# Norms of q and k from the products of W and T in place of two Gram diagonals, with ScalarE's passes in a new order

## The chip, the cores and the metric

One core of one Trainium2 chip runs the kernel. The metric is device time in microseconds, the median of several runs; the kernel before has a median of 374.44 us (three runs, 373.13 to 374.47).

## What is computed

The input x is 16 images of 192 channels and 48 x 48 pixels (N = 2304 tokens). Each image is group-normalised, goes through channel attention (8 heads of 24 channels) and is added to x:

```
qkv  = gn(x)^T @ w_qkv
q, k = q / |q|, k / |k| * temperature      # norms over the tokens, one for each channel
attn = softmax(k @ q^T)                    # 24 x 24 for each head
out  = (v @ attn^T) @ w_out + b_out
x    = x + out
```

The kernel never forms q, k or v. With G = X^T X, the 192 x 192 Gram matrix of the normalised input, and T = G W, the logits are W_k^T T_q, and the squared norm of channel c is the sum over rows of W[:, c] * T[:, c].

## The kernel before

Two images are one pair, and there are eight pairs (PAIRS). An image has 192 channels; the 2 x 192 of a pair lie in three tiles t of 128 partitions: tile 0 is the first 128 channels of image 0, tile 2 those of image 1, tile 1 the last 64 of both. Everything that goes through TensorE is split into two fp16 halves, high and low, and the products high x high, high x low and low x high are summed in PSUM.

Every engine runs `for_pairs`: a step p = -1 to 7, each with a **part A** and a **part B**. The order inside the parts is written by hand in the tables of lines 69 to 98: `PE_A[j]` is what PE does after slot j of part A, `PE_B[n]` after result n of part B, and so on for ScalarE (ACT), GpSimd (POOL) and VectorE (VEC). FIRST_ tables hold for p = -1, LAST_ tables for the end (part B of p = 6 and part A of p = 7). The engines meet only by semaphores, and each works through its own list in order.

Part A of step p has 18 slots, one for each 128 tokens of pair p+1. In slot j PE transposes into the PSUM ring `u_ps` (`transposes`, six matmuls, three slots ahead), ScalarE copies that to `tok` (`to_tok`, ring of four), and PE multiplies it (`gram`, six matmuls into `g_ps`). Between the slots stand the later steps of pair p: `flip` (transposes of the scaled logits), softmax on VectorE with `exp` on ScalarE, `attn_values` ("v", after slot 8) and `folded_weights` ("m", after slot 11). VectorE also takes the statistics of pair p+2 (`bn`).

Part B has 18 results: `result` on PE is five matmul steps of 384 columns into `u_ps` (for tile 1, results 4, 5, 10, 11, 16 and 17, mostly as pairs of 64-wide halves), and `result` on VectorE adds them to x. Result n waits until VectorE is done with result n - 4. Between them stand the steps of pair p+1: `finish_gram`, `group_sums` (for pair p+2), `gram_weights` ("w0", "w1": T into `g_ps` and bank 0 of `s_ps`), and `scores`. T is split by `high_t` on ScalarE and `low_t` on VectorE ("t0", "t1", "t2", one for each part k of the rows).

`scores` makes, for both images and both halves j of the channels, two products: T_q with W_k and W_q side by side (192 columns), and T_k with W_k (96). From the diagonals of the second and third VectorE takes the squared norms (`norms`: two multiplications by the identity, a sum, a maximum), GpSimd the power -0.5 (`norm_power`, "norms" in its table), and VectorE scales the logits (`spread`).

ScalarE also normalises pair p+2: nine chunks c of 768 columns, each as a full value `xn` ("x", `chunk_value`) and as its high half `h_sb` ("h", `chunk_high`); a bare number is both. GpSimd subtracts (`split`). The `xn` ring has three places, so x of chunk c waits for GpSimd's chunk c - 3. Chunks of tile 0 are 0, 3 and 6; they wait for results, since the h_sb that they overwrite is read by part B:

```
if str(what)[0] != "x" and t == 0:
    need(act, out_mm, (q - 2) * NO + (g + 1) * NO // GROUPS)
```

That is 6 results for chunk 0, 12 for chunk 3 and 18 for chunk 6.

## Time and profile before

| | |
|---|---|
| median of three runs | 374.44 us |
| the profiled execution | 374.76 us |
| its span, first to last instruction | 372.8 us |
| PE, matmuls | 331.2 us busy, 89% |
| PE, loads of the fixed operand | 233.4 us, 63% |
| VectorE (DVE) | 283.2 us, 76% |
| ScalarE (ACT) | 235.9 us, 63% |
| GpSimd (POOL) | 150.4 us, 40% |
| mean granted clock of TensorE | 0.980 |

How to read the rows: matmuls are pipelined, and each row's time reaches from a matmul's start to its end, which overlaps the next. What a stream of matmuls costs is read from the distance of the starts. A row of windows has its stretch and length, then for PE, PE's loads, VectorE, ScalarE and GpSimd the busy us (and the number of instructions), the granted clock (1.00 is the full 2.4 GHz, 0.50 is 1.2 GHz), the DMA engines' share and GB/s. A row of groups by line ends in | total us, mean ns of one | idle time before. On the other engines too a row's time is some 0.1 us longer than the distance to the next start.

### The profile page before, as it was taken

The numbers are of one execution on the slowest core, as the hardware profiler recorded it, in microseconds if no ns is written. First come the engines' busy times: TensorE is split into PE (matmuls) and PEld (weight loads), VectorE is DVE, ScalarE is ACT, GpSimd is POOL, SyncE is SP. The second block draws the span as 40 slices with busy tenths as digits, with TensorE's granted clock in tenths as the row PEclk, the third lists the DMA queues.
The fourth block names the chain that finished last, engine by engine and source line by source line (L and its number), as shares of the span: only waits on it lengthen the run. The fifth ranks groups of instructions, "written<-read, shape, count | busy, mean of one in ns | idle before, by whom it ended". The sixth has DMA issues, their size and how long they took to land.

```text
span 372.8 us, 9327 instructions
## 1 busy us (share of the span) xinstructions
PE 331.2 (89%) x3724; PEld 233.4 (63%) x3724; DVE 283.2 (76%) x666; ACT 235.9 (63%) x410; POOL 150.4 (40%) x133
## 2 busy tenths in 40 slices
PE   0048856999999999999999999999999999999795
PEld 0036645875778566865777577856686577765452
DVE  4889855887699669986799769966998665359774
ACT  1098489763997299747996399729974699610200
POOL 0079858301970169203950197016920395001000
PEclk9999976899999999999999999999999999999999
DMA  7999900004994279815991499427981563034766
GB/s 235 359 286 246 244 16 3 2 2 139 300 323 132 86 233 326 247 44 137 336 335 44 134 297 338 124 87 226 320 261 45 165 217 88 2 105 150 230 213 192
DMA packets 30826, 67.73 MB, mean 182 GB/s; under 512 B 5504, under 2 KB 12096, under 8 KB 30784
## 3 DMA queue, kind: packets, MB, share of 16 engines
q1 hardware_dynamic: 30544, 66.56, 56.7%
q10 hardware_dynamic: 240, 0.59, 0.6%
q8 instruction: 29, 0.48, 0.5%
q14 instruction: 13, 0.11, 0.1%
HBM read 29.38 MB, written 28.31 MB: 155 GB/s over the span
## 4 chain that ended last, share of the span: by engine, by line
PE 64%; ACT 15%; issue 10%; DVE 5%; DMA 2%; SPq 2%; POOL 1%; ACTq 0%; POOLq 0%
PE u_ps L927 30%; PE g_ps L927 17%; PE s_ps L927 10%; ACT h_sb L543 4%; ACT tok L581 4%; ACT xn L537 3%; PE u_ps L976 2%; DMA wo<-in_L_conv_w_out_dram 2%; PE u_ps L977 2%; ACT h_sb L550 1%; DVE x_sb L855 1%; PE u_ps L979 1%; PE u_ps L978 1%; SPq L354 1%; SPq L359 1%
## 5 line engine op out<-in xcount | busy, mean ns | idle before, releaser
L474 POOL TENSOR_TENSOR l_sb<-xn,h_sb 128x768 f16<-128x768 f32 x63 | 103.8, 1649 | 56.0 <-ACT h_sb L543 55.7
L855 DVE SCALAR_TENSOR_TENSOR x_sb<-u_ps,bias,x_sb 128x384 f32<-128x384 f32 x144 | 85.9, 613 | 24.2 <-PE u_ps L927 24.1
L927 PE MATMUL g_ps<-tok 128*128 128x64 f16 (+1 forms) x864 | 87.1, 241 | 3.4 <-ACT tok L581 2.9
L537 ACT ACTIVATE xn<-x_sb,rb 128x768 f32<-128x768 f32 x63 | 63.6, 1020 | 29.7 <-POOL rb L486 29.7
L581 ACT COPY tok<-u_ps 128x384 f32<-128x384 f32 x144 | 65.0, 485 | 19.8 <-PE u_ps L979 18.6
L927 PEld LDWEIGHTS g_ps<-tok 128*128 128x128 f16 x864 | 57.0, 99 | 28.5 <-ACT tok L581 5.8
L728 DVE BATCH_NORM_STATS2 bnst<-x_sb 128x6 f32<-128x384 f32 x144 | 69.9, 543 | 5.3 <-DMA x_sb<-in_x_dram 5.2
L927 PE MATMUL u_ps<-h_sb,ml 128*128 128x384 f16 (+1 forms) x336 | 73.2, 327 | 0.0
L543 ACT ACTIVATE h_sb<-x_sb,rb 128x768 f16<-128x768 f32 x63 | 64.4, 1022 | 0.0
L976 PE MATMUL u_ps<-id,h_sb 128*128 128x128 f16 x288 | 48.9, 223 | 8.2 <-DVE l_sb L718 7.4
L977 PE MATMUL u_ps<-id,l_sb 128*128 128x128 f16 x288 | 48.9, 223 | 0.0
L927 PE MATMUL u_ps<-h_sb,mh 128*128 128x384 f16 (+1 forms) x192 | 47.2, 326 | 1.5 <-DVE ml L817 1.5
L480 POOL TENSOR_TENSOR grs<-gvar,minus_half 128x3 f32<-128x3 f32 x8 | 7.1, 885 | 102.6 <-DVE gvar L761 102.6
L927 PE MATMUL u_ps<-hl,mh 128*128 128x384 f16 (+1 forms) x192 | 47.9, 334 | 0.0
L927 PE MATMUL u_ps<-l_sb,mh 128*128 128x384 f16 (+1 forms) x192 | 47.1, 326 | 0.0
L927 PEld LDWEIGHTS u_ps<-h_sb,ml 128*128 128x128 f16 (+1 forms) x336 | 28.9, 101 | 23.9 <-issue 7.3
L976 PEld LDWEIGHTS u_ps<-id,h_sb 128*128 128x128 f16 x288 | 27.4, 100 | 8.6 <-ACT h_sb L550 6.5
L978 PE MATMUL u_ps<-id,h_sb 128*128 128x128 f16 x144 | 32.1, 223 | 0.0
L979 PE MATMUL u_ps<-id,l_sb 128*128 128x128 f16 x144 | 32.1, 223 | 0.0
L977 PEld LDWEIGHTS u_ps<-id,l_sb 128*128 128x128 f16 x288 | 28.8, 100 | 0.4
L927 PEld LDWEIGHTS u_ps<-hl,mh 128*128 128x128 f16 (+1 forms) x192 | 14.7, 103 | 15.0 <-issue 7.5
L491 POOL TENSOR_TENSOR r<-n,minus_half 96x8 f32<-96x8 f32 x8 | 13.3, 1660 | 24.9 <-DVE n L771 24.2
(144 smaller groups left out, 567.6 us busy)
## 6 DMA issues: line engine op xcount, KB each, us to landing
x_sb<-in_x_dram SPq DMA_DIRECT2D x48, 384.0 KB, 5.4
...
```

The lines of the kernel that those rows point to most:

```text
L474: nc.gpsimd.tensor_tensor(l_sb[:, par, t, cols], xn[:, c % XN_RING, :], h_sb[:, par, t, cols], ALU.subtract).then_inc(l_ok, 1)
L491: nc.gpsimd.tensor_tensor(r8[:, :], n8[:, :], minus_half[0:HC, :].to_broadcast([HC, 8]), ALU.pow).then_inc(r8_ok, 1)
L537: nc.scalar.activation(xn[:, c % XN_RING, :], xcol(q, t, g * GW, GW), ACT.Identity, bias=rb[:, par, 1, t:t + 1], scale=rb[:, par, 0, t:t + ...
L543: nc.scalar.activation(h_sb[:, par, t, g * GW:g * GW + GW], xcol(q, t, g * GW, GW), ACT.Identity, bias=rb[:, par, 1, t:t + 1], scale=rb[:, ...
L581: nc.scalar.copy(tok[:, j % TOK_RING, :, :].rearrange("p b n -> p (b n)").bitcast(F32), slot_words(j)).then_inc(tok_a, 1)
L728: ins = V.bn_stats(bnst[:, t, 6 * part:6 * part + 6], xcol(q, t, part * BW, BW))
L855: V.scalar_tensor_tensor(out=xs, in0=block_ps(n), scalar=bias[:, t:t + 1], in1=xs, op0=ALU.add, op1=ALU.add).then_inc(out_ok, 1)
L927: return nc.tensor.matmul(dst, lhs, rhs, start=start, stop=stop, skip_group_check=True)
L976: nc.tensor.transpose(bank[:, b, 0:P], h_sb[:, par, 2 * b, px], id16[:, :])
L977: nc.tensor.transpose(bank[:, b, 256:384], l_sb[:, par, 2 * b, px], id16[:, :])
L978: nc.tensor.transpose(bank[:, :, P:P + C1], h_sb[:, par, 1, px], id16[:, :])
L979: nc.tensor.transpose(bank[:, :, P + C1:P + 2 * C1], l_sb[:, par, 1, px], id16[:, :]).then_inc(tr_mm, 1)
```

## The change

The norms no longer come from diagonals. After VectorE has taken the low half of T (now of its q columns only), it multiplies T in PSUM by W in place (`scalar_tensor_tensor`, 384 columns, three parts k). ScalarE copies the products to fp16 ("p", `high_products`), VectorE takes what is left ("lo", `low_products`), and PE sums over the rows: `squares` has the products as the 128-wide fixed operand (4 column groups x 3 parts x high and low, 24 matmuls) and moves two columns, `side`, that hold ones in the rows of one image or the other. `scores` keeps only the 96 x 96 products of T_q and W_k. `norms` is one instruction, the maximum. The tables move scores to result 10 (squares follow result 12), GpSimd's "norms" one chunk ahead, and ScalarE's passes: x1 and x2 ahead of the copies of T, x7 out of part B and behind slot 1 of part A, x8 and h8 to slots 3 and 5, ahead of exp.

```diff
-PE_B = {0: ["gram"], 2: ["sums"], 4: ["w0"], 6: ["w1"], 12: ["scores"]}
-ACT_A = {0: ["h6"], 2: ["h7"], 4: ["x8"], 6: ["exp", "h8"], 11: ["v"], 14: ["m"]}
-ACT_B = ["x0", "t0", "t1", "t2", "h0", 1, 2, 3, 4, 5, "x6", "x7"]
-POOL_B = ["power", 0, 1, 2, 3, 4, "norms", 5, 6, 7, 8]
+PE_B = {0: ["gram"], 2: ["sums"], 4: ["w0"], 6: ["w1"], 10: ["scores"], 12: ["squares"]}
+ACT_A = {0: ["h6"], 1: ["x7"], 2: ["h7"], 3: ["x8"], 5: ["h8"], 6: ["exp"], 11: ["v"], 14: ["m"]}
+ACT_B = ["x0", "x1", "x2", "t0", "t1", "t2", "h0", "h1", "p", "h2", 3, 4, 5, "x6"]
+POOL_B = ["power", 0, 1, 2, 3, "norms", 4, 5, 6, 7, 8]
 VEC_A = {0: ["soft_in"], 3: ["soft_out"], 7: ["v"], 11: ["m0"], 13: ["m1"], 17: ["stats"]}
-VEC_B = {0: ["gram"], 2: ["var"], 4: ["z"], 6: ["t0", "t1", "t2"], 12: ["norms"], 17: ["spread", "bn", "bn", "bn", "bn"]}
+VEC_B = {0: ["gram"], 2: ["var"], 4: ["z"], 6: ["t0", "t1", "t2"], 9: ["lo"], 12: ["norms"], 17: ["spread", "bn", "bn", "bn", "bn"]}
...
-FIRST_ACT_B = [0, "x1", "t0", "t1", "t2", "h1", 2, 3, 4, 5, "x6", "x7"]
-FIRST_POOL_B = ["power", 0, 1, 2, 3, 4, "norms", 5, 6, 7, 8]
+FIRST_ACT_B = [0, "x1", "t0", "t1", "t2", "h1", "x2", "p", "h2", 3, 4, 5, "x6"]
+FIRST_POOL_B = ["power", 0, 1, 2, 3, "norms", 4, 5, 6, 7, 8]
...
-FIRST_VEC_B = {0: ["gram", "var", "z", "t0", "t1"], 1: ["t2", "bn", "bn", "wo", "norms", "spread", "bn", "bn"]}
+FIRST_VEC_B = {0: ["gram", "var", "z", "wo", "t0", "t1"], 1: ["t2", "bn", "bn", "lo", "norms", "bn", "bn", "spread"]}
...
-LAST_PE_B = {0: ["gram"], 2: ["w0"], 3: ["w1"], 5: ["scores"], 10: ["flip"], 16: ["v"]}
+LAST_PE_B = {0: ["gram"], 2: ["w0"], 3: ["w1"], 6: ["scores"], 7: ["squares"], 11: ["flip"], 16: ["v"]}
 LAST_ACT_A = {0: ["m"]}
-LAST_ACT_B = ["t0", "t1", "t2", "exp", "v"]
+LAST_ACT_B = ["t0", "t1", "t2", "p", "exp", "v"]
...
-        tq = sb("tq", [P, 3, 2, 2 * C], F16)
-        dg = sb("dg", [HC, 8, HC])
+        tq = sb("tq", [P, 3, 2, C], F16)
+        pw16 = sb("pw16", [P, 3, 2, 2 * C + P - HC], F16)
+        side = sb("side", [P, 3, 2], F16)
...
-        qk_ps = s_ps[0:HC, :, 0:2 * C].rearrange("p b (j s c) -> p b j s c", j=2, s=2)
-        kk_ps = g_ps[0:HC, 0, 0:2 * C].rearrange("p (b j c) -> p b j c", b=2, j=2)
+        qk_ps = s_ps[0:HC, 1, 0:2 * C].rearrange("p (b j c) -> p b j c", b=2, j=2)
+        def t_ps(k):
+
+            return g_ps[:, k, 0:2 * C] if k < 2 else s_ps[:, 0, 0:2 * C]
+
+        n_ps = s_ps[:, 0, 5 * HC:5 * HC + 8]
...
-                nc.scalar.copy(tq[:, k, 0, :], src[:, 0:2 * C]).then_inc(th_ok, 1)
-
-            small_steps = {"t0": lambda q: high_t(q, 0), "t1": lambda q: high_t(q, 1), "t2": lambda q: high_t(q, 2),
+                nc.scalar.copy(tq[:, k, 0, :], src[:, 0:C]).then_inc(th_ok, 1)
+
+            def high_products(q):
+
+                need(act, n_mm, q)
+                for k in range(3):
+                    act.wait_ge(pw_ok, 3 * q + k + 1)
+                    nc.scalar.copy(pw16[:, k, 0, 0:2 * C], t_ps(k)).then_inc(ph_ok, 1)
...
-                one = id32[0:HC, 0:HC].unsqueeze(1).unsqueeze(1).to_broadcast([HC, 2, 2, HC])
-                ch = Chain(dve, diag, q * DIAG, DIAG)
-                V.tensor_tensor(dg[:, 4:8, :].rearrange("p (b j) c -> p b j c", b=2), qk_ps[:, :, :, 0, :], one, ALU.mult)
-                ch.then(V.tensor_tensor(dg[:, 0:4, :].rearrange("p (b j) c -> p b j c", b=2), kk_ps, one, ALU.mult))
-                ch.then(V.tensor_reduce(n8[:, :], dg[:, :, :], AX_X, ALU.add))
-                ch.then(V.tensor_scalar(n8[:, :], n8[:, :], NORM_EPS ** 2 * NORM_FACTOR, None, ALU.max))
-
-            def spread(q):
-
-                dve.wait_ge(r8_ok, q + 1)
-                V.tensor_tensor(qk_s[:, :, :].rearrange("p (b j) c -> p b j c", b=2), qk_ps[:, :, :, 1, :],
+                V.tensor_tensor(qk_s[:, :, :].rearrange("p (b j) c -> p b j c", b=2), qk_ps,
...
-                V.tensor_tensor(tq[:, k, 1, :], src[:, 0:2 * C], tq[:, k, 0, :], ALU.subtract).then_inc(tl_ok, 1)
+                V.tensor_tensor(tq[:, k, 1, :], src[:, 0:C], tq[:, k, 0, :], ALU.subtract).then_inc(tl_ok, 1)
+                dve.wait_ge(tl_ok, 3 * q + k + 1)
+                V.scalar_tensor_tensor(out=src[:, 0:2 * C], in0=src[:, 0:2 * C], scalar=W_SCALE, in1=(w1 if k == 2 else w0)[:, 0:2 * C],
+                                       op0=ALU.mult, op1=ALU.mult).then_inc(pw_ok, 1)
+
+            def low_products(q):
+                for k in range(3):
+
+                    dve.wait_ge(ph_ok, 3 * q + k + 1)
+                    V.tensor_tensor(pw16[:, k, 1, 0:2 * C], t_ps(k), pw16[:, k, 0, 0:2 * C], ALU.subtract).then_inc(pl_ok, 1)
...
-                        for dst, lc, rc in ((qk_ps[:, b, j, :, :], qc, None), (kk_ps[:, b, j, :], kc, kc)):
-                            def cols(w):
-                                return w[:, rc] if rc else w.rearrange("p (s c) -> p s c", s=2)[:, :, qc]
-
-                            terms = [(tq[:, b, 0, lc], wh0[:, :]), (tq[:, b, 1, lc], wh0[:, :]), (tq[:, b, 0, lc], wl0[:, :]),
-                                     (tq[:, 2, 0, lc], wmh[:, b, :]), (tq[:, 2, 1, lc], wmh[:, b, :]),
-                                     (tq[:, 2, 0, lc], wml[:, b, :])]
-                            for k, (lhs, w) in enumerate(terms):
-                                last = mm(dst, lhs, cols(w), k == 0, k == 5)
+                        terms = [(tq[:, b, 0, qc], wh0[:, kc]), (tq[:, b, 1, qc], wh0[:, kc]), (tq[:, b, 0, qc], wl0[:, kc]),
+                                 (tq[:, 2, 0, qc], wmh[:, b, kc]), (tq[:, 2, 1, qc], wmh[:, b, kc]),
+                                 (tq[:, 2, 0, qc], wml[:, b, kc])]
+                        for k, (lhs, w) in enumerate(terms):
+                            last = mm(qk_ps[:, b, j, :], lhs, w, k == 0, k == 5)
                 last.then_inc(s_mm, 1)
+
+            def squares(q):
+
+                pe.wait_ge(pl_ok, 3 * q + 3)
+                for a in range(4):
+                    c = C - C * (a // 2) + HC * (a % 2)
+                    terms = [(pw16[:, k, i, c:c + P], side[:, k, :]) for k in range(3) for i in (0, 1)]
+                    dst = n_ps.rearrange("p (s b j) -> p s j b", s=2, b=2)[:, a // 2, a % 2, :]
+                    for k, (lhs, one) in enumerate(terms):
+                        last = mm(dst, lhs, one, k == 0, k == len(terms) - 1)
+                last.then_inc(n_mm, 1)
```

ScalarE from the start of a steady part B to x3 (`xn` rows are "x", `h_sb` rows are "h", `tq` the high halves of T, `pw` those of the products), before:

```order
L537 ACTIVATE xn<-x_sb,rb 128x768 [waits l_ok,norm]
L626 CAST tq<-g_ps 128x384 [waits t_mm] x2
L626 CAST tq<-s_ps 128x384 [waits t_mm]
L543 ACTIVATE h_sb<-x_sb,rb 128x768 [waits out_mm]
L537 ACTIVATE xn<-x_sb,rb 128x768 [waits l_ok]
L543 ACTIVATE h_sb<-x_sb,rb 128x768
L537 ACTIVATE xn<-x_sb,rb 128x768 [waits l_ok]
L543 ACTIVATE h_sb<-x_sb,rb 128x768
L537 ACTIVATE xn<-x_sb,rb 128x768 [waits l_ok,out_mm]
```

and now:

```order
L545 ACTIVATE xn<-x_sb,rb 128x768 [waits l_ok,norm]
L545 ACTIVATE xn<-x_sb,rb 128x768 [waits l_ok] x2
L634 CAST tq<-g_ps 128x192 [waits t_mm] x2
L634 CAST tq<-s_ps 128x192 [waits t_mm]
L551 ACTIVATE h_sb<-x_sb,rb 128x768 [waits out_mm]
L551 ACTIVATE h_sb<-x_sb,rb 128x768
L641 CAST pw<-g_ps 128x384 [waits pw_ok,n_mm]
L641 CAST pw<-g_ps 128x384 [waits pw_ok]
L641 CAST pw<-s_ps 128x384 [waits pw_ok]
L551 ACTIVATE h_sb<-x_sb,rb 128x768
L545 ACTIVATE xn<-x_sb,rb 128x768 [waits l_ok,out_mm]
```

x1 and x2 stand ahead of the copies of T; behind h0 and h1 the three copies of products are new; x3 still waits for `out_mm`, the results.

ScalarE at the end of part B and in the first slots of part A (`tok` rows are the slots' copies, the row out of `s_ps` is exp), before:

```order
L537 ACTIVATE xn<-x_sb,rb 128x768 [waits l_ok] x2
L581 COPY tok<-u_ps 128x384 [waits gram_mm,tr_mm]
L543 ACTIVATE h_sb<-x_sb,rb 128x768 [waits out_mm]
L581 COPY tok<-u_ps 128x384 [waits gram_mm,tr_mm] x2
L543 ACTIVATE h_sb<-x_sb,rb 128x768
L581 COPY tok<-u_ps 128x384 [waits gram_mm,tr_mm] x2
L537 ACTIVATE xn<-x_sb,rb 128x768 [waits l_ok]
L581 COPY tok<-u_ps 128x384 [waits gram_mm,tr_mm] x2
L587 ACTIVATE s_ps<-s_ps 96x96 [waits soft]
L543 ACTIVATE h_sb<-x_sb,rb 128x768
```

and now:

```order
L589 COPY tok<-u_ps 128x384 [waits gram_mm,tr_mm]
L551 ACTIVATE h_sb<-x_sb,rb 128x768 [waits out_mm]
L589 COPY tok<-u_ps 128x384 [waits gram_mm,tr_mm]
L545 ACTIVATE xn<-x_sb,rb 128x768 [waits l_ok]
L589 COPY tok<-u_ps 128x384 [waits gram_mm,tr_mm]
L551 ACTIVATE h_sb<-x_sb,rb 128x768
L589 COPY tok<-u_ps 128x384 [waits gram_mm,tr_mm]
L545 ACTIVATE xn<-x_sb,rb 128x768 [waits l_ok]
L589 COPY tok<-u_ps 128x384 [waits gram_mm,tr_mm] x2
L551 ACTIVATE h_sb<-x_sb,rb 128x768
L589 COPY tok<-u_ps 128x384 [waits gram_mm,tr_mm]
L595 ACTIVATE s_ps<-s_ps 96x96 [waits soft]
```

One x (x7) left part B and stands behind the second copy; five passes instead of three are now ahead of exp, four of them ahead of the fifth copy instead of two.

PE in a steady part B from result 10's halves to result 12 (`u_ps` rows are results, `wh,tq` scores), now:

```order
L952 MATMUL s_ps<-wml,tq 96x96
L952 MATMUL u_ps<-hl,mh 64x384 [waits out_ok]
L952 MATMUL u_ps<-hl,mh 64x384
L952 MATMUL u_ps<-h_sb,mh 64x384 x2
L952 MATMUL u_ps<-l_sb,mh 64x384 x2
L952 MATMUL u_ps<-h_sb,ml 64x384 x2
L952 MATMUL u_ps<-h_sb,ml 128x384
L952 MATMUL u_ps<-h_sb,mh 128x384 [waits hl_in2,out_ok]
L952 MATMUL u_ps<-l_sb,mh 128x384
L952 MATMUL u_ps<-hl,mh 128x384
L952 MATMUL u_ps<-h_sb,ml 128x384 x2
L952 MATMUL s_ps<-side,pw 128x2 [waits pl_ok]
```

Result 11 (first row after a score's last) stands behind the 24 scores, and the squares behind result 12, waiting for `pl_ok`; before, scores followed result 12.

## Rows read from the trace of the kernel before

**Rows 1.** Window of one period, from the start of a part B.

```profile
121.41:161.86 40.45, 40.37 (x469) 28.30 (x468) 32.91 (x80) 29.91 (x51) 17.97 (x14) 1.00 0.64 206
```

**Rows 2.** Part 4 of the page: the chain that ended last.

```profile
PE 64%; ACT 15%; issue 10%; DVE 5%; DMA 2%; SPq 2%; POOL 1%; ACTq 0%; POOLq 0%
```

**Rows 3.** Timeline of PE, scores (start, us, engine, line, forms, count).

```profile
136.74 0.33 PE L927 MATMUL s_ps<-wh,tq 128*96 128x192 f16 x2
...
137.23 0.25 PE L927 MATMUL g_ps<-wh,tq 128*96 128x96 f16 x2
...
137.50 0.33 PE L927 MATMUL s_ps<-wh,tq 128*96 128x192 f16 x2
...
139.79 0.33 PE L927 MATMUL u_ps<-h_sb,mh 128*128 128x384 f16 x1
```

**Rows 4.** Timeline of PE, group sums of that part B.

```profile
124.68 0.32 PE L927 MATMUL u_ps<-parts,grp 128*128 128x6 bf16 x7
```

**Rows 5.** Timeline of PE, results 10 to 12 and a transpose.

```profile
134.33 0.35 PE L927 MATMUL u_ps<-hl,mh 128*64 128x384 f16 x2
...
135.93 0.33 PE L927 MATMUL u_ps<-h_sb,mh 128*128 128x384 f16 x1
...
144.09 0.22 PE L976 MATMUL u_ps<-id,h_sb 128*128 128x128 f16 x1
```

**Rows 6.** Timeline of ScalarE in part B; idle before, and releaser, in brackets.

```profile
130.96 0.86 ACT L626 CAST tq<-g_ps 128x384 f16<-128x384 f32 x2 [2.02 <-PE g_ps L927]
...
136.72 1.01 ACT L537 ACTIVATE xn<-x_sb,rb 128x768 f32<-128x768 f32 x1
```

**Rows 7.** Timeline of ScalarE, first slots of part A.

```profile
144.62 0.48 ACT L581 COPY tok<-u_ps 128x384 f32<-128x384 f32 x1 [0.46 <-PE u_ps L979]
145.00 1.03 ACT L543 ACTIVATE h_sb<-x_sb,rb 128x768 f16<-128x768 f32 x1
145.93 0.85 ACT L581 COPY tok<-u_ps 128x384 f32<-128x384 f32 x2
...
147.59 0.86 ACT L581 COPY tok<-u_ps 128x384 f32<-128x384 f32 x2
...
149.98 0.26 ACT L587 ACTIVATE s_ps<-s_ps 96x96 f32<-96x96 f32 x1
...
151.06 1.24 ACT L581 COPY tok<-u_ps 128x384 f32<-128x384 f32 x3
```

**Rows 8.** Timeline of PE, Gram of slots 1, 3 and 7; values.

```profile
146.45 0.62 PE L927 MATMUL g_ps<-tok 128*128 128x384 f16 x6
...
148.12 0.61 PE L927 MATMUL g_ps<-tok 128*128 128x384 f16 x6
...
151.60 0.62 PE L927 MATMUL g_ps<-tok 128*128 128x384 f16 x6
...
153.16 0.25 PE L927 MATMUL s_ps<-wvh,ax 96*96 96x192 f16 x1
```

**Rows 9.** Timelines of ScalarE and VectorE, one period earlier: softmax.

```profile
109.53 0.26 ACT L587 ACTIVATE s_ps<-s_ps 96x96 f32<-96x96 f32 x1
...
111.80 0.56 DVE L808 TENSOR_TENSOR ax<-s_ps,ax 96x384 f16<-96x384 f32 x1
```

**Rows 10.** Groups by line and form, VectorE and TensorE's loads.

```profile
L817 DVE SCALAR_TENSOR_TENSOR ml<-s_ps,mh 128x384 f16<-128x384 f32 x8 | 4.4, 545 | 3.5 <-ACT mh L598 3.5
...
L817 DVE SCALAR_TENSOR_TENSOR ml<-s_ps,mh 64x192 f16<-64x192 f32 x16 | 5.6, 349 | 0.6 <-ACT mh L603 0.5
...
L927 PEld LDWEIGHTS u_ps<-h_sb,ml 128*128 128x128 f16 x240 | 23.4, 98 | 21.5 <-issue 7.3 <-DVE x_sb L855 0.3
```

**Rows 11.** Timeline of VectorE: the norms' last instruction, twice.

```profile
142.03 0.21 DVE L771 TENSOR_SCALAR n<-n 96x8 f32<-96x8 f32 x1
...
337.90 0.17 DVE L771 TENSOR_SCALAR n<-n 96x8 f32<-96x8 f32 x1
```

**Rows 12.** Window in the first part A.

```profile
66.00:68.00 2.00, 2.00 (x18) 1.49 (x17) 1.57 (x5) 1.81 (x3) 1.24 (x1) 0.50 0.00 0
```

More of the change, by code:

```diff
@@ L673, in _ @@
             V.memset(wl1[C1:P, :], 0.0)
+            V.memset(pw16[:, :, :, 2 * C:], 0.0)
+            ones = ((0, slice(0, P), 0), (1, slice(0, P), 1), (2, slice(0, C1), 0), (2, slice(C1, P), 1))
+            for k, rows, b in ones:
+                V.memset(side[rows, k, b:b + 1], 1.0)
+                V.memset(side[rows, k, 1 - b:2 - b], 0.0)
             for z in (wmh, wml):
@@ L1166, in _ @@
             small_steps = {"gram": finish_gram, "w0": lambda q: gram_weights(q, False),
-                           "w1": lambda q: gram_weights(q, True), "scores": scores, "flip": flip,
+                           "w1": lambda q: gram_weights(q, True), "scores": scores, "squares": squares, "flip": flip,
                            "v": attn_values, "m": folded_weights}
```

22 lines of the change are left out of this document (14 added, 8 removed).

## The prediction

> **What bounds the kernel now.** I first cut the span at the start of each part B. From 80.96 to 323.66 seven of these starts lie 40.45 us apart, and in each of the six windows PE is busy for 40.37 us at the full granted clock, as in the one shown [rows 1]. So six of the eight pairs run in a steady rhythm that TensorE paces, and a start-up and an end stand around them. The chain that ended last is PE for 64% and ScalarE for 15% [rows 2]. That second share matters: a PE that looks busy in this table may still be starting its matmuls late, because the durations overlap. So I went on to the timelines and read starts, not ends.
>
> In part B the scores take PE from 136.74 to 139.79, 3.05 us, with nothing waited for [rows 3]. The 18 results stand five matmuls apart at 0.81 us (135.93 to 136.74) [rows 3, 5]. Part B is pure throughput. In part A it is different: slot j's Gram matmuls start 0.52 us after the start of its token copy on ScalarE wherever that copy is late. Slots 1, 3 and 7 are such (copies at 145.93, 147.59, 151.06; Gram matmuls at 146.45, 148.12, 151.60) [rows 7, 8]. The other slots take 0.78 to 0.79 us. So ScalarE already delays PE a little here, and one more pass among the first slots is paid in full.
>
> **Scores and squares on PE.** Six score matmuls with 96 columns on either side take 0.27 us (137.23 to 137.50), 0.045 each [rows 3]. Now all 24 are of this form: 1.08 us. Added are 24 matmuls with a 128-wide fixed operand and two moving columns. The nearest row is the seven group sums, the same fixed operand with six columns: 0.32 us from the first start to the last end, of which one matmul lasts 0.165, so 0.026 each [rows 4]; 24 are 0.63 us. Scores now stand between results 10 and 11, which use 64-wide halves, and a change of width costs about 0.1: from 134.33 to 135.93 there are nine steps of 0.163, 1.47 us, in 1.60 [rows 5]. Two more changes: 0.2. Part B on PE shortens by 3.05 - 1.08 - 0.63 - 0.20 = 1.14 us.
>
> The cost of a square is bounded by 0.026 and, above, by 0.098, the load of a 128-wide operand if it were not hidden behind other work [rows 10]; I take the lower, because the seven sums load just such operands and keep 0.026. The Trainium skill, TensorE: Matmul & The Clock Gate, section "Wait — 56ns, not 53.3ns?", gives two floors for small matmuls, 25 ns, or 62 ns where the sequencer decodes in its own code. By the second, 24 squares would be an estimated 1.5 us; the trace agrees with the first.
>
> **VectorE in part B.** The four norm instructions go; their last ends at 142.24, some 2.2 us after the scores, and 2.1 of that is their own work [rows 3, 11]. Added are three products in place of 0.55 us each, and three low halves of 0.55; the three low halves of T shrink from 0.55 to 0.35 (192 columns) [rows 10]. That is 3.3 + 1.1 - 1.7 - 2.1 = +0.6 us on an engine busy for 33 of 40 [rows 1]. Where it sits matters more. The T block starts about 131.3 and lasts 3 x 0.9 = 2.7 us instead of 1.5, so result 7 is added from 134.0, 1.2 later than before. PE needs that only for result 11, four results on and behind the scores: hidden. Results 7, 8, 9 and the three low halves end near 137.1; PE reaches the squares when result 12 is out, 136.74 + 1.28 = 138.0 [rows 3]. Hidden too, with 0.9 us to spare. If that cover went, PE would wait at the squares for what is missing.
>
> **ScalarE in part B.** x1 and x2 now fill its wait before t0 at 130.96 (2 us long, 1.84 needed) [rows 6]. The product copies cost 3 x 0.38, the smaller T copies save 0.5. It would reach x3 near 136.0. But x3 (chunk 3, tile 0) waits until twelve results are out of PE. Before, result 11 ended at 136.09 (result 12 starts 135.93, the last matmul 0.16 earlier and 0.33 long), and x3 started at 136.72, unhindered [rows 5, 6]. Now the scores are ahead of result 11: 136.09 + 1.08 + 0.20 = 137.37. **This is a new wait of 1.3 us.** Seven passes follow at 0.92 (h6, from 145.00 to 145.93, is one) [rows 7], to 143.82. The first token copy of part A stood at 144.62 because PE's transposes began at 144.09 [rows 5, 7]. It could start at 143.48 by PE, and starts at 143.82 by ScalarE. Part B gives 0.80 us, not 1.14.
>
> **ScalarE in part A.** x7 has moved here, behind slot 1, and x8 and h8 come earlier. Counting from copy 0, with 0.37 per copy and 0.92 per pass [rows 7]: h6 at 0.38, copy 1 at 1.31, x7 at 1.67, copy 2 at 2.6, h7, copy 3 at 3.9, x8, copies 4 and 5 at 5.2 and 5.55, h8, copy 6 at 6.85, exp at 7.2. Before, copy 2 stood at 1.7, copy 3 at 2.97 and exp at 5.36 (149.98). The Gram matmuls come 0.52 after their copy or 0.79 after the slot before: slot 2 at 3.1, slot 3 at 4.4, slot 4 at 5.7, slot 8 at 8.95. Before, slot 7 stood at 6.98, so slot 8 at 7.77 [rows 8]. That is 1.18 us lost.
>
> Behind slot 8 PE would start the attention values at 9.7. They wait for VectorE's softmax, which needs 2.83 us from exp (109.53) to the end of the low half of ax (112.36) [rows 9]: 7.2 + 2.83 = 10.05, so they start at 10.1. Before it was 153.16 - 144.62 = 8.54. **Part A loses 1.56 us.** What follows on PE is its own throughput; ml1 and the channel statistics are 1.8 us later on VectorE against 1.56 on PE, inside the 0.5 us that VectorE waited at part B's start.
>
> GpSimd gets "norms" one chunk earlier; split 4 then ends about 144.4 and x7, which waits for it, starts at 145.5. SP's DMAs are not moved, and the longer rhythm gives them time.
>
> A steady pair: +1.56 - 0.80 = +0.76 us. Part A of pairs 1 to 6 and part B of pairs 0 to 5 make six: **+4.6 us**.
>
> **The start.** In the first part B ScalarE gives up x7 (0.92) and 0.4 of the T copies and takes 1.1 for products: about -0.1. In the first part A the granted clock is 0.5, the lower level, until 68, and PE gets through 18 matmuls in 2 us [rows 12], a slot and a half. Its slots are so long that they hide x7: +0.1 to +0.2 at the attention values. Together +0.1.
>
> **The end.** The last part B, from 323.66, is a dependent chain: scores, norms, power, spread, flip, softmax, values, folded weights. Its norms end at 338.07 [rows 11]. Now scores start one result later (+0.81) and are 1.97 shorter; a result and the squares follow (+0.81 + 0.63) with two changes of width (+0.2); one norm instruction stands for four (-2.05); and the low halves are some 0.15 late. That is 1.4 us earlier. It shrinks in the queues of results that all hooks now stand one place further back in: the flip behind result 11, the softmax behind results 10 to 13. I get values and folded weights 1.0 us earlier, between 0.5 and 1.4.
>
> **Sum.** 4.6 + 0.1 - 1.0 = +3.7 us. The profiled execution took 374.76, 0.3 over the median, so 378.5 there and **378.1 us** for the median.
>
> **Rivals.**
> - *The ring of four token slots hides ScalarE in part A.* Then only gains stay: 6 x -0.80 - 1.0 = -5.8, 368.6 us: faster. It decides as soon as the copies of slots 2 to 7 may be a slot late without moving a Gram start. Against: in slots 1, 3 and 7 the start follows the copy by 0.52 [rows 7, 8], and copies 2, 3 and 4 now come 0.9 to 1.5 us later. Chance 0.10.
> - *Both small waits fail to appear.* x3 finds its result, and the softmax is in time. A loses 1.18, B gains 1.14: six times +0.04, and -0.9 around it: 373.7 us. For: both waits are under 0.4 us past another limit. Against: both were found with starts that the trace gives to 0.05. Chance 0.17.
> - *The squares cost more than the sums did, because their loads stand in the open.* At 0.098 each they take 2.35 us, 1.72 more; PE's transposes then start later than before and bind again (tok0 +0.58): 6 x (1.56 + 0.58) + 0.7 = +13.5, 388 us. Against: the sums [rows 4]. Chance 0.07. (With the 62 ns of the Trainium skill's page the estimate would be 382 us.)
> - The order of the instructions shows that the change does what it says; no chance is kept for that.
>
> **How the numbers follow.** My case has the remaining 0.66. Its own range is 375.5 to 381: per pair 0.3 to 1.1 us, the end's bounds, and up to 0.8 either way in the start, whose idle times move with the clock. For 8 in 10 I leave out the first rival, the last, and a rest of 0.03: 373.4 to 381.5. A measurement of this kernel can tell 0.5%, 1.9 us, from no change. Slower: 0.62 of my case, 0.01 of the second rival, 0.07 of the third, 0.70. Same: 0.04 + 0.14 = 0.18. Faster: 0.10 + 0.02 = 0.12.
>
> **What would show it.** A period of 41.2 us between starts of part B; 24 squares in about 0.65 us and scores in 1.1; ScalarE idle for 1.3 us before xn (x3) with the results' matmuls as releaser; Gram starts of slots 2 to 4 each about 1.3 us apart; values waiting 0.4 us for ax. The forecast is wrong if the period is under 40.4, if slots of part A keep 0.8 us, or if PE waits in part B for the low halves of the products.

## The result, and the profile after

The changed kernel took **377.48 us** (median of 12 executions, 375.94 to 380.15), the kernel before on the same chip 374.00 (372.62 to 374.68). The ratio is **1.0117, with a 95% interval of 1.0093 to 1.0140**: slower by 1.2% (3.5 us between the medians; the ratio is estimated over the executions and is not the quotient of the medians). Ratios leave out the executions that are over 1.5% above the fastest of the same kernel; the medians are of all. The forecast was 378.1 and slower. The steady part came out as worked. In the profiled execution the start came out 1.9 us lower and the end 3.4 us higher than forecast, so it is in part luck that the median lies only 0.6 us from the forecast.

| | before | after |
|---|---|---|
| profiled execution, its span | 374.76, 372.8 us | 380.15, 378.3 us |
| first TensorE transposes | 23.78 | 22.90 |
| first steady part B | 80.96 | 79.19 |
| steady period, and how many | 40.45, six | 41.27, six |
| part B start to first token copy ("tok0") | 23.21 | 22.50 |
| tok0 to the next part B ("part A") | 17.24 | 18.77 |
| last part B start to the end of the span | 49.1 | 51.5 |
| mean granted clock | 0.980 | 0.968 |

First the busy times from the top of the page, and the window of one period as in [rows 1]:

```profile
PE 327.2 (86%) x3724; PEld 222.7 (59%) x3724; DVE 285.7 (76%) x699; ACT 242.8 (64%) x434; POOL 148.8 (39%) x133
```

```profile
120.46:161.73 41.27, 39.75 (x469) 26.90 (x467) 33.54 (x83) 30.82 (x54) 17.72 (x14) 1.00 0.62 202
```

TensorE is busy for 0.62 us less in a period that is 0.82 us longer. It was 99.8% busy before; now it stands still for 1.52 us a period, and the clock is not the cause, since it is 1.00 here. So I looked for TensorE's waits, which the table of waits of TensorE in the changed kernel gives (us in total, times, longest):

```profile
PE g_ps L952 <- ACT tok L589: 10.8, 25, 2.9
...
PE s_ps L952 <- DVE ax L824: 3.2, 8, 1.9
```

Before, the first of these rows was one wait of 2.9 us, and the second one of 1.0. The timeline of TensorE in one part B shows what the engine saved (scores, result 11, squares, result 13, first transposes):

```profile
134.15 0.29 PE L952 MATMUL s_ps<-wh,tq 128*96 128x96 f16 x2
...
135.36 0.35 PE L952 MATMUL u_ps<-hl,mh 128*64 128x384 f16 x2
...
137.12 0.74 PE L952 MATMUL s_ps<-side,pw 128*128 128x2 f16 x24
137.72 0.32 PE L952 MATMUL u_ps<-h_sb,mh 128*128 128x384 f16 x1
...
142.01 0.22 PE L1001 MATMUL u_ps<-id,h_sb 128*128 128x128 f16 x1
```

The scores take 1.21 us to the start of result 11, a change of width in them, against 3.05 in [rows 3]. The 24 squares take 0.60 us (137.12 to 137.72), 0.025 each. The transposes for part A start 21.55 us after the part's start (142.01 - 120.46) against 22.68 before (144.09 - 121.41, [rows 5, 1]): 1.13 us sooner. But ScalarE's timeline in the same place shows the new wait before x3, and a row of passes without a gap up to tok0 (142.96):

```profile
136.51 1.03 ACT L545 ACTIVATE xn<-x_sb,rb 128x768 f32<-128x768 f32 x1 [1.51 <-PE u_ps L952]
...
142.96 0.46 ACT L589 COPY tok<-u_ps 128x384 f32<-128x384 f32 x1
143.32 1.03 ACT L551 ACTIVATE h_sb<-x_sb,rb 128x768 f16<-128x768 f32 x1
144.25 0.46 ACT L589 COPY tok<-u_ps 128x384 f32<-128x384 f32 x1
144.61 1.03 ACT L545 ACTIVATE xn<-x_sb,rb 128x768 f32<-128x768 f32 x1
145.54 0.46 ACT L589 COPY tok<-u_ps 128x384 f32<-128x384 f32 x1
```

Of the 1.13 us only 0.71 reach the token copy. The last four rows are part A as changed: a copy, a pass of 0.92, a copy, a pass of 0.92. TensorE's Gram matmuls in the same stretch follow that rhythm:

```profile
144.76 0.61 PE L952 MATMUL g_ps<-tok 128*128 128x384 f16 x6
146.05 0.61 PE L952 MATMUL g_ps<-tok 128*128 128x384 f16 x6 [0.34 <-ACT tok L589]
147.35 0.61 PE L952 MATMUL g_ps<-tok 128*128 128x384 f16 x6 [0.34 <-ACT tok L589]
148.64 0.61 PE L952 MATMUL g_ps<-tok 128*128 128x384 f16 x6 [0.34 <-ACT tok L589]
149.43 0.60 PE L952 MATMUL g_ps<-tok 128*128 128x384 f16 x6
...
153.00 0.28 PE L952 MATMUL s_ps<-wvh,ax 96*96 96x192 f16 x1 [0.19 <-DVE ax L824]
```

Slots 2, 3 and 4 start 1.29 us apart, then it is 0.79 again. The bracket (0.34) is only the engine's empty time; what counts is the distance of the starts, since the matmuls of a slot stretch over it. The values start 10.04 us after tok0, before it was 8.54 [rows 8, 7].

Last the windows of the final part B of the changed kernel, where the kernel before shows a clock of 1.00 up to its last results (columns as in [rows 1]; the last three are granted clock, DMA share and GB/s):

```profile
348.00:350.00 2.00, 0.91 (x11) 0.92 (x12) 1.97 (x4) 0.18 (x1) 0.00 (x0) 1.00 0.75 215
350.00:352.00 2.00, 2.00 (x17) 1.09 (x15) 1.75 (x5) 0.77 (x2) 0.00 (x0) 0.69 0.95 373
352.00:354.00 2.00, 2.00 (x18) 1.63 (x18) 0.43 (x1) 0.41 (x1) 0.00 (x0) 0.50 0.21 48
...
358.00:360.00 2.00, 2.00 (x8) 0.88 (x6) 1.02 (x2) 0.00 (x0) 0.00 (x0) 0.50 0.04 8
360.00:362.00 2.00, 2.00 (x10) 0.96 (x8) 0.84 (x2) 0.00 (x0) 0.00 (x0) 0.75 0.47 184
```

For some ten microseconds the granted clock is at its lower level, 1.2 GHz, and TensorE gets through 8 to 10 instructions in 2 us of results where, in the windows behind these, it does 14 to 21 at full clock. What went before it is in TensorE's timeline:

```profile
349.09 0.28 PE L952 MATMUL s_ps<-wvh,ax 96*96 96x192 f16 x1 [1.86 <-DVE ax L824]
```

The kernel before waits 0.96 us at this place.

### The profile page after: what moved, and what is told of

Same layout as the page of the kernel before. It is cut to its first block, busy times and chain, and to the rows that moved or that the text cites. A ratio compares the mean times of both kernels' runs of the same rounds, so it can differ in the third digit from the quotient of the medians.

```text
span 378.3 us, 9399 instructions
## 1 busy us (share of the span) xinstructions
PE 327.2 (86%) x3724; PEld 222.7 (59%) x3724; DVE 285.7 (76%) x699; ACT 242.8 (64%) x434; POOL 148.8 (39%) x133
## 4 chain that ended last, share of the span: by engine, by line
PE 55%; ACT 24%; DVE 9%; issue 6%; DMA 2%; SPq 2%; POOL 0%; ACTq 0%; POOLq 0%
PE u_ps L952 25%; PE g_ps L952 14%; PE s_ps L952 11%; ACT h_sb L551 10%; ACT xn L545 8%; ACT tok L589 5%; DMA x_sb<-in_x_dram 2%; PE u_ps L1001 2%; PE u_ps L1002 2%; DVE s_ps L821 1%; DVE ax L824 1%; DVE ax L823 1%; SPq L362 1%; DVE bnst L748 1%; PE u_ps L1003 1%
## 5 line engine op out<-in xcount | busy, mean ns | idle before, releaser
L482 POOL TENSOR_TENSOR l_sb<-xn,h_sb 128x768 f16<-128x768 f32 x63 | 102.6, 1646 | 54.9 <-ACT h_sb L551 54.1
L880 DVE SCALAR_TENSOR_TENSOR x_sb<-u_ps,bias,x_sb 128x384 f32<-128x384 f32 x144 | 87.1, 615 | 31.0 <-PE u_ps L952 30.8
L952 PEld LDWEIGHTS g_ps<-tok 128*128 128x128 f16 x864 | 56.1, 99 | 37.9 <-ACT tok L589 16.6
L589 ACT COPY tok<-u_ps 128x384 f32<-128x384 f32 x144 | 66.1, 476 | 16.0 <-PE u_ps L1004 13.8
L952 PE MATMUL u_ps<-h_sb,ml 128*128 128x384 f16 (+1 forms) x336 | 74.6, 332 | 0.0
L952 PE MATMUL u_ps<-h_sb,mh 128*128 128x384 f16 (+1 forms) x192 | 47.7, 329 | 1.5 <-DVE ml L833 1.5
L952 PE MATMUL u_ps<-l_sb,mh 128*128 128x384 f16 (+1 forms) x192 | 47.7, 329 | 0.0
```

The source lines that it names most:

```text
L482: nc.gpsimd.tensor_tensor(l_sb[:, par, t, cols], xn[:, c % XN_RING, :], h_sb[:, par, t, cols], ALU.subtract).then_inc(l_ok, 1)
L589: nc.scalar.copy(tok[:, j % TOK_RING, :, :].rearrange("p b n -> p (b n)").bitcast(F32), slot_words(j)).then_inc(tok_a, 1)
L880: V.scalar_tensor_tensor(out=xs, in0=block_ps(n), scalar=bias[:, t:t + 1], in1=xs, op0=ALU.add, op1=ALU.add).then_inc(out_ok, 1)
L952: return nc.tensor.matmul(dst, lhs, rhs, start=start, stop=stop, skip_group_check=True)
```

## Experiments

The theory after the result: ScalarE's passes in part A cost 1.5 us a pair; in part B its new wait for result 11 eats part of what TensorE saves; squares and products on their own cost nothing beyond what is counted. The rivals: that the added work of TensorE and VectorE is the loss, that the ring hides ScalarE, that the clock at the end is all of it. Except where it says otherwise, an edit is made to the changed kernel.

**x7 back in part B.** The tables of ScalarE; the steady ones are shown, and x7 goes back in the first part B too:

```diff
-ACT_A = {0: ["h6"], 1: ["x7"], 2: ["h7"], 3: ["x8"], 5: ["h8"], 6: ["exp"], 11: ["v"], 14: ["m"]}
-ACT_B = [..., "h2", 3, 4, 5, "x6"]
+ACT_A = {0: ["h6"], 2: ["h7"], 4: ["x8"], 6: ["exp", "h8"], 11: ["v"], 14: ["m"]}
+ACT_B = [..., "h2", 3, 4, 5, "x6", "x7"]
```

> The change, with x7 back at the end of ScalarE's list for part B and x8, exp, h8 at their old slots. My theory (ScalarE's order in part A costs 1.5 us a pair, and x3's wait for result 11 eats half of what PE saves in part B): part A falls from 18.77 back to 17.24 us, the first token copy comes 0.92 later (one more pass behind x3's wait), so the period is 22.50 + 0.92 + 17.24 = 40.66 us; 6 x -0.61 = -3.7: about 373.8 us, level with the kernel before. Rival 1 (the added squares and VectorE products cost the time, not ScalarE's order): the period stays at 41.2 or grows, 377 to 382 us. Rival 2 (the lower granted clock at the end is the whole loss): only the end would matter, period near 41.3.

Measured 381.97 us, ratio 1.0219 (1.0183 to 1.0255). **A miss by 8 us.** Part A is back at 17.21 us, as forecast. But tok0 comes 24.19 us after part B's start, not 23.42, and three of the six periods are a further 1.0 to 1.2 us longer. ScalarE's timeline at the end of a part B:

```profile
144.89 1.03 ACT L545 ACTIVATE xn<-x_sb,rb 128x768 f32<-128x768 f32 x1 [0.67 <-POOL l_sb L482]
145.83 0.45 ACT L589 COPY tok<-u_ps 128x384 f32<-128x384 f32 x1
```

x7 waits 0.67 us for GpSimd. The buffer xn that x7 fills is the one that split 4 reads, and GpSimd's timeline has the norms, which the change moved ahead of split 4, in its way:

```profile
141.31 1.66 POOL L499 TENSOR_TENSOR r<-n,minus_half 96x8 f32<-96x8 f32 x1
143.06 0.20 POOL L503 TENSOR_TENSOR rk<-r,temp 96x4 f32<-96x4 f32 x1
143.21 3.25 POOL L482 TENSOR_TENSOR l_sb<-xn,h_sb 128x768 f16<-128x768 f32 x2
```

The longer periods have another cause. There TensorE has finished its first transposes and stands still for 1.99 us until the late copy, and this is what follows (first its timeline, then the windows):

```profile
187.75 0.61 PE L952 MATMUL g_ps<-tok 128*128 128x384 f16 x6 [1.99 <-ACT tok L589]
```

```profile
186.00:188.00 2.00, 0.25 (x4) 0.19 (x5) 1.72 (x4) 1.70 (x3) 1.87 (x2) 1.00 0.86 232
188.00:190.00 2.00, 1.99 (x26) 1.54 (x25) 0.90 (x2) 2.00 (x4) 1.30 (x1) 0.84 0.96 237
190.00:192.00 2.00, 2.00 (x18) 1.55 (x16) 1.90 (x6) 1.99 (x5) 1.97 (x2) 0.50 1.00 399
192.00:194.00 2.00, 2.00 (x27) 1.58 (x26) 0.40 (x2) 1.24 (x4) 0.01 (x1) 0.80 1.03 359
```

The clock falls 1.6 us after the pause, and part A takes 18.36 us instead of 17.21. In two more periods it falls likewise, once as the pause ends. The other three have the same pause (1.98 to 1.99 us) and no such fall. The three slow parts A are the three with the fall; that the pause brings it is inferred from where it stands, since no run here takes this pause away alone.

**Scores behind result 11.** So that x3's releaser no longer stands behind them:

```diff
-PE_B = {0: ["gram"], 2: ["sums"], 4: ["w0"], 6: ["w1"], 10: ["scores"], 12: ["squares"]}
+PE_B = {0: ["gram"], 2: ["sums"], 4: ["w0"], 6: ["w1"], 11: ["scores"], 12: ["squares"]}
```

> The change, with the scores behind result 11 in place of result 10, so that x3's releaser does not stand behind them. My theory: ScalarE's wait before x3 falls from 1.5 us to under 0.1, and ScalarE no longer sets the first token copy; PE's own transposes do, which I put 0.34 us ahead of it. Period 41.27 - 0.34 = 40.93, 6 x -0.34 = -2.0: 375.5 us. Rival (PE sets the first token copy already, x3's wait is hidden): the wait goes and the period stays 41.27, 377.5 us. Second rival (no such PE bound): the whole 1.5 is gained, period 39.8, 369 us.

Measured 374.24 us, ratio 1.0031 (1.0003 to 1.0059). The wait is 0.18 us, tok0 comes at 21.83 and part A keeps 18.79: period 40.62, a little better than the 40.93 forecast (the time was forecast at 375.5). ScalarE's timeline shows that it now waits for TensorE:

```profile
133.92 1.03 ACT L545 ACTIVATE xn<-x_sb,rb 128x768 f32<-128x768 f32 x1 [0.18 <-PE u_ps L952]
...
141.03 0.48 ACT L589 COPY tok<-u_ps 128x384 f32<-128x384 f32 x1 [0.57 <-PE u_ps L1004]
```

So both bounds of tok0 were as the prediction had them, ScalarE with the wait and TensorE just behind it. TensorE's transposes start 21.30 us after part B's start instead of 21.55. I put that down to a change of width less, now that the scores stand between a result in 64-wide halves and one of full width; no run takes it apart.

**Both edits.**

> Both edits together: x7 back at the end of part B and the scores behind result 11. My theory: part A 17.24; in part B ScalarE loses 1.5 us of waiting and gets 0.92 of work, so that PE's own throughput sets the first token copy at 22.16 us: period 39.4, 6 x -1.87 = -11.2, 366.3 us, faster than both kernels by 2% or more. Rival (gains do not add, since VectorE's longer T block or the squares bind next): period 40.3 or more, 372 us or more.

Measured 374.10 us, ratio 0.9996 (0.9960 to 1.0032). Another miss, by 8 us: period 40.07 (22.85 + 17.21) for the 39.4 forecast, with one of six 0.4 longer. The period alone is worth 4 us of the miss. x7 waits 0.66 us for split 4 here too. Its executions spread from 369.6 to 375.7, with mean clocks from 0.979 to 0.958.

**The kernel before, with ScalarE's new part A alone.** An edit to the kernel before: ACT_A as in the change, x7 taken out of both lists of part B.

> The kernel before, with ScalarE's part A as in the change alone (x7 behind slot 1, x8, h8 one or more slots earlier, exp behind h8) and x7 gone from part B. My theory: part A grows from 17.24 to 18.8 us, the slots of the Gram matmuls 2 to 4 going to about 1.3 us each; part B stays at 23.21 to the first token copy because PE's transposes set it there; period 42.0, six times +1.55 = +9.3: 383.3 us. Rival (the ring of four token slots hides the passes): same time, 374 us. Rival (part B gains the 0.92 that ScalarE gives up): period 41.1, 378 us.

Measured 382.18 us, ratio 1.0236 (1.0193 to 1.0278). The period is 42.00 in all six: 23.21 to tok0, 18.79 from there. This is the loss of part A by itself, without a score, a square or a product changed. TensorE's timeline has the same three slots 1.29 us apart:

```profile
145.18 0.62 PE L927 MATMUL g_ps<-tok 128*128 128x384 f16 x6
146.48 0.61 PE L927 MATMUL g_ps<-tok 128*128 128x384 f16 x6 [0.34 <-ACT tok L581]
147.77 0.61 PE L927 MATMUL g_ps<-tok 128*128 128x384 f16 x6 [0.34 <-ACT tok L581]
149.06 0.62 PE L927 MATMUL g_ps<-tok 128*128 128x384 f16 x6 [0.34 <-ACT tok L581]
```

The rival of the hiding ring is out. So is the one by which part B gives back ScalarE's 0.92: ScalarE waits 1.37 us for the transposes before tok0.

**Both edits, and GpSimd's norms behind split 4.**

```diff
-POOL_B = ["power", 0, 1, 2, 3, "norms", 4, 5, 6, 7, 8]
+POOL_B = ["power", 0, 1, 2, 3, 4, "norms", 5, 6, 7, 8]
```

(and FIRST_POOL_B likewise.)

> The last but one run (x7 back in part B, scores behind result 11) and GpSimd's norms back behind split 4, where the kernel before has them. Its trace showed ScalarE idle for 0.66 us before x7 with split 4's low half as releaser: x7 reuses the slot of xn that split 4 reads, and the norms (1.9 us) stand ahead of that split. Theory: the wait goes, the first token copy comes 22.19 us after the start of part B instead of 22.85, part A stays 17.21, period 39.40, six times -0.67 = -4.0: 370 us (1% faster than the kernel before). Rival: the norms, two passes of GpSimd later, make the flip of the scores late, and PE waits there instead: period 40 or more, 374 us.

Measured **370.07 us, ratio 0.9906 (0.9872 to 0.9940)**: the forecast of 370, and faster than both kernels. x7's wait is gone and nobody waits for the flip. Where nothing disturbs it, tok0 comes at 22.09 and the period is 39.3 (22.09 + 17.21). That is 1.15 us under the 40.45 of the kernel before. TensorE's transposes come at 21.30, as with the scores behind result 11 alone, and would allow a tok0 of 21.83; ScalarE, with a gapless row of passes from x3 to x7, keeps the other 0.26. Four of the six periods are 0.4 to 0.7 longer, and VectorE's timeline names the next limit:

```profile
115.78 1.02 DVE L748 BATCH_NORM_STATS2 bnst<-x_sb 128x6 f32<-128x384 f32 x2 [1.05 <-DMA x_sb<-in_x_dram]
...
155.78 1.02 DVE L748 BATCH_NORM_STATS2 bnst<-x_sb 128x6 f32<-128x384 f32 x2 [1.21 <-DMA x_sb<-in_x_dram]
```

The statistics now wait for the next images. In the steady periods the changed kernel has no such wait, and the kernel before one, of 0.30 us. In the longer periods VectorE takes this lateness into part B's results, for which TensorE then waits up to 0.64 us. That the input bounds them was read, not tested.

**exp ahead of h8.**

```diff
-5: ["h8"], 6: ["exp"]
+5: ["exp"], 6: ["h8"]
```

> The change, with exp of the softmax one pass earlier in part A, ahead of h8, and h8 behind slot 6. Theory: the values wait 0.34 us for ax in the change, because exp stands behind h8; exp 0.92 earlier takes that wait away and moves no Gram matmul (copy 7 comes 7.5 us after copy 0, and slot 7 starts at 8.1). Period 41.27 - 0.34 = 40.93, six times: -2.0, 375.5 us. Rival (the ring makes slot 8 late when h8 stands behind slot 6): period 41.27 or more.

Measured 374.58 us, ratio 1.0037 (1.0008 to 1.0066). Part A takes 18.27 us, 0.50 less than in the change and not 0.34: copy 6 is also earlier, so that slots 5 to 8 are all 0.78 apart. Slots 2 to 4 keep their 1.29. Two of its six periods, 41.03 and 41.05 beside 40.76, are again those with a wait of the statistics for the images. Of the 1.53 us lost in part A, 0.5 thus come from exp and copy 6 standing behind h8, and the remaining 1.0 from the passes between copies 1 and 4. Which of these passes costs how much was not separated.

**Squares twice.** The run with the scores behind result 11, and

```diff
-                    terms = [(pw16[:, k, i, c:c + P], side[:, k, :]) for k in range(3) for i in (0, 1)]
+                    terms = [(pw16[:, k, i, c:c + P], side[:, k, :]) for k in range(3) for i in (0, 1)] * 2
```

> The run with scores behind result 11 and x7 in part A (PE sets its first token copy at 21.83 us), with each square matmul issued twice in the same accumulation: 48 instead of 24, so the norms are those of doubled squares. Theory (a square costs 0.026 us in place, its operand's load is hidden): first token copy at 21.83 + 0.62 = 22.45, period 40.62 + 0.62 = 41.24, about 377.9 us. Rival (0.098 us each, loads in the open): +2.35 a period, 388 us. Rival (62 ns each): +1.5, 383 us.

Measured 377.08 us (one execution). tok0 comes at 22.43 instead of 21.83, and the period is 41.23, forecast 41.24. 24 more squares cost 0.60 us, 0.025 each, where TensorE sets the pace:

```profile
137.11 1.34 PE L952 MATMUL s_ps<-side,pw 128*128 128x2 f16 x48
138.31 0.32 PE L952 MATMUL u_ps<-h_sb,mh 128*128 128x384 f16 x1
```

Now the clock at the end. In the profiles that keep the change's last part B, the stretch from its start to the end of the span is 47.7 us where the clock stays at 1.00 (both edits; exp first), 49.4 with one fall of some 3 us (x7 back; scores behind result 11; the best version) and 51.5 in the changed kernel's own profile. That TensorE pauses before the values for 1.86 us holds for all six of them (1.85 with exp first). The next runs ask whether TensorE's pause before the values brings the fall.

**Values behind result 17, in the best version and in the change.**

```diff
-LAST_PE_B = {..., 11: ["flip"], 16: ["v"]}
+LAST_PE_B = {..., 11: ["flip"], 17: ["v"]}
```

(and VectorE's "v" of the last part from 15 to 16.)

> The same, and in the last part B the attention values behind result 17 in place of 16, so that PE's idle stretch before them is one result (0.81 us) shorter and the next one longer. The changed kernel's profile has 1.86 us of idle PE there and the granted clock at 0.50 some 2 us behind it, for 9 us. Theory (the long idle stretch brings the fall): no fall at the end, 1 to 3 us less than the run without this edit in the executions that fall, and never a slower one. Rival (the fall comes from the thin work of the whole stretch, however it is cut): same time as without the edit, and a fall in some executions as before.

Measured 371.83 us, ratio 0.9952 (0.9914 to 0.9990), beside 370.07 without the edit: no gain, though its profile has no fall at the end. Its executions spread from 368.2 to 373.5 us, and those of the best version from 367.9 to 374.0, so that the case stayed open. It was asked again in the change, together with the change itself.

> The changed kernel itself, unaltered, as the other end of the comparison for the two that follow. Its twelve earlier executions lay in three groups by mean granted clock: 0.98 (376.3 us), 0.976 (377.5) and 0.968 (379.7). Theory: these are executions with no, a short and a long fall of the clock in the last part B; period 41.27 in all of them, and from the last start of part B to the end of the span 47.7 us without a fall, 49.4 with a short one, 51.5 with a long one. Rival (the groups come from the start, whose inputs arrive at different times): the end is alike in all and the start differs by 1 to 3 us.

Measured 379.34 us, ratio 1.0159 (1.0126 to 1.0192), six executions: one at clock 0.98 (376.51), one at 0.972 (377.69), four at 0.967 to 0.968 (379.3 to 380.7). The period is 41.27 in its profile too, and the end 50.7 us, with two falls of 3.4 us each. But the rival is not out: the first steady part B starts at 80.61 here and at 79.19 in the first profile, 1.4 us apart for one and the same kernel. Of this, 0.8 us are later first transposes (23.71 against 22.90), and 0.6 us the first part A (19.42 against 18.79), in which the clock came back to full at 67.7 and not at 64. So the spread of the times comes from both ends, and a mean clock does not tell at which of them it was low.

> The change, with the last pair's attention values behind result 17 in place of 16, nothing else: PE's idle stretch ahead of them 0.94 us in place of 1.86. Theory (that stretch brings the fall at the end): no fall, all executions at a clock of 0.975 or more, median 376.3 us, 1.2 less than the change. Rival (it does not, as the run with all edits suggests, whose clocks still reached 0.954): the same three groups and 377.5 us.

Measured 380.07 us, ratio 1.0187 (1.0163 to 1.0212), beside 379.34 for the change on the same chip. **The theory in this form is refuted.** The fall is there all the same:

```profile
348.77 0.28 PE L952 MATMUL s_ps<-wvh,ax 96*96 96x192 f16 x1 [0.94 <-DVE ax L824]
351.28 0.26 PE L952 MATMUL s_ps<-woh,vh 96*128 96x192 f16 x1 [1.32 <-DVE vl L830]
```

```profile
352.00:354.00 2.00, 1.77 (x18) 1.11 (x15) 0.56 (x1) 0.68 (x2) 0.00 (x0) 0.52 0.53 126
```

The edit cuts one pause in two and leaves the idle time as it is: 0.94 and 1.32 us where there was 1.86.

**Filler in the pause.** Eleven matmuls that nothing reads, in the last pair only; they are added work, and the computation is otherwise whole.

```diff
             def attn_values(q):
+                if isinstance(q, int) and q == PAIRS - 1:
+                    for _ in range(11):
+                        mm(g_ps[:, 0, 0:2 * C], wh0[:, 0:P], wh0[:, :], True, True)
```

> The change, with eleven matmuls of 384 columns on constant operands, into a PSUM bank that nothing reads any more, put into PE's 1.86 us of idle time ahead of the last pair's attention values. They compute nothing that is used. Theory (PE's idle time there brings the fall): PE has no gap left there, no fall at the end, median 376.3 us or a little more if the last filler ends late (up to 0.2). Rival (the fall comes whatever PE does there): the same groups as the change, 377.5 us.

Measured 376.77 us, ratio 1.0115 (1.0088 to 1.0141), beside 379.34 for the change on the same chip: 2.6 us less between medians of six executions each, for more work. (The first twelve executions of the change had a median of 377.48 and a ratio to the kernel before of 1.0117, hardly above the filler's.) The profile has the filler where the pause was, and full clock behind it:

```profile
347.00 1.96 PE L952 MATMUL g_ps<-wh 128*128 128x384 f16 x11
348.93 0.28 PE L952 MATMUL s_ps<-wvh,ax 96*96 96x192 f16 x1
```

```profile
350.00:352.00 2.00, 1.89 (x20) 1.20 (x19) 1.83 (x4) 0.61 (x2) 0.00 (x0) 1.00 0.85 336
352.00:354.00 2.00, 1.05 (x18) 0.68 (x15) 1.03 (x3) 1.35 (x4) 0.00 (x0) 1.00 0.30 68
```

One of its six executions is still at 379.13 with a clock of 0.968; of the eighteen of the change, eight are above 379. A fall thus seems rarer and is not ruled out, but one in six against eight in eighteen is thin evidence. The profile alone is no proof either: of the eight profiles with the pause of 1.86 us, only the changed kernel's two have a fall directly behind it (1.7 and 0.5 us after its end); the other six have none there.

**Filler in the best version.**

> The best version so far (x7 in part B, scores behind result 11, norms behind split 4; 370.07 us, 0.9906 of the kernel before) with the eleven filler matmuls ahead of the last pair's attention values. Theory: the filler takes 1 to 2.6 us off, as it did in the change (376.77 against 379.34 on one chip): 368 to 369 us, ratio 0.984 to 0.988. From the last start of part B to the span's end 47.7 to 47.9 us, with the clock at 1.00 throughout. Rival (in this version other falls of the clock and late inputs set the spread): 370 us, ratio 0.991.

Measured **367.54 us (367.13 to 369.73), ratio 0.9847 (0.9825 to 0.9869)**: 1.5% faster than the kernel before and the best of all. The time is a little under the 368 to 369 forecast, the ratio in its range, but the profile is not as forecast: it shows a fall at the end after all and takes 49.4 us from the last start of part B, as the best version does without the filler. It is also the slowest of its six executions. How often the others fall is not seen in a trace, and what the filler gained here is seen in none; the intervals of the ratios with and without it (0.9825 to 0.9869, 0.9872 to 0.9940) just fail to overlap.

This profile also shows what the filler cannot reach. TensorE has a second pause in the last part B, of 1.54 us, before the first result that takes the last pair's folded weights, and it is here that the clock falls:

```profile
346.48 0.32 PE L952 MATMUL u_ps<-h_sb,mh 128*128 128x384 f16 x1 [1.54 <-DVE ml L833]
```

```profile
346.00:348.00 2.00, 1.52 (x6) 0.78 (x7) 0.43 (x3) 0.37 (x2) 0.00 (x0) 0.71 0.82 237
348.00:350.00 2.00, 2.00 (x8) 0.95 (x7) 1.02 (x2) 0.00 (x0) 0.00 (x0) 0.50 0.38 89
```

That pause is in every profile, the kernel before's included. The short falls that make an end of 49.4 us (x7 back, scores behind result 11, the best version, this run) all begin within 0.5 us of its end, and so does the second fall of the change run again. They are 5.7 us and more behind the pause before the values, so a filler there does not answer for them; one in the second pause was not tried.

## Why the prediction came out as it did

- **Part A, +1.56 a pair: measured +1.53.** The token copies follow the passes in the order counted, Gram slots 2 to 4 stand 1.29 apart, the values start at 10.04 after tok0 (forecast 10.1) and wait for ax (1.13 us behind slot 8, where a slot takes 0.78). Made alone in the kernel before, the same edit gives +1.55 and a period of 42.00. Shown.
- **Part B on TensorE, -1.14: measured -1.13.** Scores 1.08 and a change of width, measured 1.21 together; squares 0.63, measured 0.60; in place, 24 more squares cost 0.60. The higher floor of the Trainium skill's page (TensorE: Matmul & The Clock Gate, section "Wait — 56ns, not 53.3ns?"), 62 ns, which it gives for decoding in the sequencer's own code, is not seen here; the measured 0.025 us agrees with its lower one, 25 ns.
- **The new wait of x3, 1.3 us: measured 1.51**, and tok0 -0.71 where -0.80 stood. With the scores one result later the wait is 0.18 and tok0 gains 0.67. Shown. TensorE would have allowed tok0 about 0.4 us sooner than ScalarE did (142.01 + 0.53 against 142.96).
- **VectorE's longer T block, hidden:** its low halves end at 135.99, TensorE reaches the squares at 137.12 and does not wait there in the steady part, with 1.1 us to spare. Only in the first part B, where TensorE has no results to fill the time, it waits 0.75 us. Right.
- **The period, +0.76: measured +0.82**, six times 4.9 us where 4.6 stood.
- **The start, +0.1: measured -1.8, of which -0.3 is the change's. This term was wrong, though by little.** 0.88 of it is no effect of the change: the first transposes come at 22.90 against 23.78 in the two profiles, and between 22.2 and 24.2 in the others, as the inputs arrive. ScalarE's part up to tok0 is -0.28 (37.50 us after those transposes, against 37.78), where -0.1 was counted; the prediction's own figures, -0.92, -0.4 and +1.1, add up to -0.2. The rest, -0.61, is from tok0 to the first steady part B, 18.79 us instead of 19.40, and this is no effect of the change either: the clock was back at full some 4 us sooner (64 in place of 68, [rows 12]). In the second profile of the changed kernel, with the clock back at 67.7, the same stretch takes 19.42. So the step "its slots are so long that they hide x7" is right (+0.02 where +0.1 to +0.2 was counted), and the time of the clock's return, which stood in the range and not in the sum, moves the start by 0.6 us.
- **The end, -1.0: measured +2.4 in the profiled execution. This term was wrong too, and the mechanism was missing.** The chain itself did better than forecast: 47.7 us in the versions without a fall against 49.1, -1.4, the upper bound. What the sum left out is the clock. It fell for ten microseconds in the changed kernel's profile, 1.7 us behind a pause of 1.86 us that was 0.96 before. I had read the pauses of the start for the clock and not those of the end, though the change takes work from TensorE there while its wait grows. What the fall costs is shown (51.5 against 47.7). That the longer pause brings it is not: the same pause stands without a fall behind it in six other profiles, and only the filler's times, one of six above 379 against eight of eighteen, speak for it. The twelve executions lie in three groups: 376.3 us at a mean clock of 0.98, 377.5 at 0.976, 379.8 at 0.968. That these are no, a short and a long fall at the end is inferred, and the start has a part in it, as the second profile shows.
- **The sum** was +3.7 and became, for the profiled pair, 4.9 - 1.8 + 2.4 = +5.5 of span (378.3 - 372.8), and +3.5 in the medians. With the end without a fall, and the start without the difference in arrival, it would be 4.9 - 0.9 - 1.4 = +2.6 (0.6 of the 0.9 is the clock's early return); the lowest group, 376.3 against 374.0, is +2.3.
- **My own follow-up failed once:** I held that x7 could go back for one pass of 0.92. The prediction had noted that x7 waits for split 4 and that the norms now come first; I used that in part A, where it cost nothing, and forgot it in part B, where it costs 0.67 and comes with a pause of TensorE of 1.99 us, in three of six cases followed by a fall of the clock.
